# Three weight loads of the opening issued by ScalarE instead of the sync engine, in a graph-network kernel

## The chip, the cores and the metric

The program runs on one core of a Trainium2 chip. The metric is the device time of one execution in microseconds (us). Below, PE is TensorE's matmul side and PEld its weight load, DVE is VectorE, ACT is ScalarE, POOL is GpSimd and SP is the sync engine. "SPq" and "ACTq" are the instruction streams of SP and ACT where they issue transfers.

## What is computed

Four layers, each followed by a residual sum and a layer norm, over 32 graphs of 256 nodes with 256 features and one 256 x 256 adjacency. The first is a gated recurrent graph layer of three steps. The opening, which this change is about, is its first step on the first two graphs:

```python
h = x
for _ in range(T):                       # T = 3
    a_in = jnp.einsum('nm,bmd->bnd', in_mat, h)      # in_mat = out_mat = adj
    a_out = jnp.einsum('nm,bmd->bnd', out_mat, h)
    av = jnp.concatenate([a_in, a_out], axis=-1)
    z = sigmoid(_lin(av, w3_w, w3_b) + _lin(h, u3_w, u3_b))
    r = sigmoid(_lin(av, w4_w, w4_b) + _lin(h, u3_w, u3_b))
    hv = tanh(_lin(av, w5_w, w5_b) + _lin(r * h, u5_w, u5_b))
    h = (1.0 - z) * h + z * hv
```

Then come a linear attention-like layer with Wq, Wk, Wv, and two graph convolutions (weights called w2 and w3s in the kernel, with biases).

## The kernel before

Each engine has an instruction list written out by hand; semaphores join them. The graphs go in 16 pairs. A pair's data is 128 partitions x 1024 floats (512 KB). Two pairs are in flight: one in the "front" lane (tiles `f_...`, state `hf_...`) and one in the "back" lane (`b_...`, `hb_...`). Each engine runs `start()`, a loop, and `finish()`. Every fp32 product is made of three products of a high and a low part: ACT copies the high part (`..._hi`), DVE subtracts it from the source (`..._lo`), PE multiplies.

The opening loads the adjacency, the first pair, all weights and the bias rows. Their landing places are tiles that are free at that time, and the trace calls them by those names:

| transfer | tile in the trace | KB |
|---|---|---|
| adj | adj_nat | 256 |
| first pair | x_front | 512 |
| u3 | b_cand (first half) | 256 |
| w4 | b_z | 512 |
| w3 | b_gate | 512 |
| w5 | b_kept | 512 |
| u5 | b_cand (second half) | 256 |
| wv, w2 | normed | 256 each |
| wq, wk | hb_feat | 256 each |
| five bias vectors | bias_rows | 1 each |

In time, PE does this at the start: 13 transposes of the identity (L953), which nothing reads; `prepare(0)`, which transposes adj (L519); `turn_first`, which transposes the pair (L544); `prepare(1)`, which transposes u3 (L519); `mix(front, 0, k)`, 24 matmuls of adj with the pair (L489); `base`, the products with u3; the bias rows' transpose (L526); `prepare(2)` to `prepare(5)` for w4, w3, w5, u5, between products. `mix` needs `hf_node_lo`, which DVE makes (L1515) from `hf_node_hi`, which ACT makes from x_front. ACT's list opens with the bias transfers (L967), a table load, `prep_hi(0)` (adjT_hi), then two copies of x_front to `hf_node_hi`. DVE halves w4, w3 and w5 in place first (`sum_halves`, L1408).

POOL waits for w5's load before it issues `bias_out`:

```python
pool.wait_ge(s_load["w5"], 16)
```

SP's list is, after the loads, the second pair's load, its 32 x 32 blocks (`x_blocks`), and a copy of the state (`input_t`).

Of the kernel before, what the change touches and what calls it, by code (L numbers as in the profile page):

```python
# [21 lines left out]
P = 128  # L22
# [133 lines left out]
def build(nc, x, adj, w3_w, w3_b, u3_w, u3_b, w4_w, w4_b, w5_w, w5_b, u5_w, u5_b, wq, wk, wv,  # L156
# [14 lines left out]
    with ExitStack() as ctx:  # L171
# [3 lines left out]
        def sem(name):  # L175
            return ctx.enter_context(nc.semaphore(name))
# [83 lines left out]
        w3_nat, w4_nat, w5_nat = back.gate[:], back.z[:], back.kept[:]  # L260
        flat = lambda t: t[:].rearrange("p g c d -> p (g c) d")
        halves = lambda t: (t[:, 0].rearrange("p (c d) -> p c d", c=C), t[:, 1].rearrange("p (c d) -> p c d", c=C))
        u3_nat, u5_nat = halves(back.cand)
# [6 lines left out]
        s_load = {n: sem("s_load_" + n) for n in ("adj", "u3", "w4", "w3", "w5", "u5", "qk", "v", "l23", "bias", "bias_out")}  # L270
# [10 lines left out]
        def upto(n, k=1):  # L281
            return 2 * n + k + 1


        def ln(q, j, g):
            return 8 * q + 2 * j + g + 1
# [14 lines left out]
        def later(n):  # L301

            return not (isinstance(n, int) and n == 0)
# [4 lines left out]
        @block.sync  # L308
        def _(sp):
            def rows(w):  # L310
                return w.rearrange("(c p) d -> p c d", p=P)

            sp.dma_start(adj_nat[:], rows(adj)).then_inc(s_load["adj"], 16)
            sp.dma_start(x_front[:], x_pairs[0]).then_inc(s_x_front, 16)
            sp.dma_start(u3_nat, rows(u3_w)).then_inc(s_load["u3"], 16)
            sp.dma_start(w4_nat, rows(w4_w)).then_inc(s_load["w4"], 16)
            sp.dma_start(w3_nat, rows(w3_w)).then_inc(s_load["w3"], 16)
            sp.dma_start(w5_nat, rows(w5_w)).then_inc(s_load["w5"], 16)
            sp.dma_start(u5_nat, rows(u5_w)).then_inc(s_load["u5"], 16)
            sp.dma_start(wv_nat, rows(wv)).then_inc(s_load["v"], 16)  # L320
            sp.dma_start(wq_nat, rows(wq)).then_inc(s_load["qk"], 16)
            sp.dma_start(wk_nat, rows(wk)).then_inc(s_load["qk"], 16)
            sp.dma_start(w2_nat, rows(l2_w)).then_inc(s_load["l23"], 16)
            sp.dma_start(w3s_nat, rows(l3_w)).then_inc(s_load["l23"], 16)

            def load_front(p):

                if not later(p - 1):
                    sp.wait_ge(s_in_turned, upto(0))
                sp.wait_ge(state_f.s_node_lo, upto(2 * p - 2))  # L330
                sp.dma_start(x_front[:], x_pairs[p]).then_inc(s_x_front, 16)

            def load_blocks(p):

                if later(p - 1):
                    sp.wait_ge(state_f.s_feat, upto(2 * p - 2))
                for b in range(4):
                    sp.dma_start(x_blocks[32 * b:32 * b + 32].rearrange("k c (r i) -> k c r i", i=32),
                                 x_turnable[p, b]).then_inc(s_x_blocks, 16)

            def keep_input(p):

                sp.wait_ge(state_f.s_feat, upto(2 * p))
                if later(p):
                    sp.wait_ge(main.s_residual, upto(p - 1))
                sp.dma_start(input_t[:], state_f.feat[:]).then_inc(s_input_t, 16)

            def keep_last_input():

                sp.wait_ge(state_f.s_feat, upto(2 * LAST))  # L350
                sp.wait_ge(state_f.s_node_lo, upto(2 * LAST))
                sp.dma_start(last_pair.input_t, state_f.feat[:]).then_inc(s_input_t, 16)

            def move_blocks(S, turn):

                sp.wait_ge(S.s_blocks, 2 * turn)
                sp.dma_start(S.scratch.rearrange("b i a n -> (b i) a n"), S.blocks).then_inc(S.s_written, 16)
                sp.wait_ge(S.s_written, 16 * turn)
                for a in range(4):
                    sp.dma_start(S.moved[32 * a:32 * a + 32],  # L360
                                 S.scratch[:, :, a].rearrange("b i n -> i b n")).then_inc(S.s_moved, 16)

            def move_sum(Y, q):

                sp.wait_ge(Y.s_sum_blocks, upto(q))
                sp.dma_start(Y.scratch.rearrange("b i a n -> (b i) a n"), Y.sum_blocks).then_inc(Y.s_sum_written, 16)
                sp.wait_ge(Y.s_sum_written, 16 * q + 16)
                for a in range(4):
                    sp.dma_start(Y.sum_moved[32 * a:32 * a + 32],
                                 Y.scratch[:, :, a].rearrange("b i n -> i b n")).then_inc(Y.s_sum_moved, 16)  # L370

            def store(Y, q):
                sp.wait_ge(Y.s_normed, ln(q, 3, 1))
                sp.dma_start(out_pairs[q + Y.pair_before], Y.result[:]).then_inc(s_stored, 16)

            def store_graph(Y, q, g):
                sp.wait_ge(Y.s_normed, ln(q, 3, g))
                sp.dma_start(out_pairs[q + Y.pair_before][:, g], Y.result[:, g]).then_inc(s_stored, 16)

            load_front(1)  # L380
            load_blocks(1)
            keep_input(0)
            with sp.Fori(1, LAST) as p:
                load_front(p + 1)
                load_blocks(p + 1)
                keep_input(p)
                move_sum(main, p - 1)
                move_blocks(state_f, p)
                store(main, p - 1)
            keep_last_input()  # L390
            for Y, q, g in ((main, LAST - 1, 0), (last_pair, 0, 0), (main, LAST - 1, 1), (last_pair, 0, 1)):
                store_graph(Y, q, g)
            sp.wait_ge(s_stored, 16 * (PAIRS + 2))
# [568 lines left out]
        def _(act):  # L962
            def copy(dst, src):
                return act.activation(dst, src, ACT.Copy)  # L964

            for i, b in enumerate((w3_b, u3_b, w4_b, w5_b, u5_b)):
                act.dma_start(bias_rows[C * i:C * i + C], b.rearrange("(c p) -> c p", p=P)).then_inc(s_load["bias"], 16)  # L967

# [1162 lines left out]
```

## Time and profile before

| | us |
|---|---|
| median of 3 runs (1244.99 to 1246.29) | 1244.99 |
| profiled execution, its own time | 1243.87 |
| span of the profiled execution | 1242.1 |
| PE busy | 1221.6 (98%) |
| DVE busy | 1047.6 (84%) |
| ACT busy | 607.4 (49%) |
| POOL busy | 193.0 (16%) |

The span runs from the first to the last instruction; the time of an execution is a little more. A busy share is an average over the whole span. Times in the rows below count from the start of the span.

### The profile page before, as it was taken

Reading aid. Unit: us, or ns where it says so; the run is one execution under the profiler, and the core shown is the slowest. Engines: PE = TensorE matmul, PEld = TensorE weight load, DVE = VectorE, ACT = ScalarE, POOL = GpSimd, SP = SyncE. Lnnn points to the kernel's source line nnn. Section 1 sums busy time; section 2 is a strip of 40 time slices with the busy share of each in tenths; the row PEclk is TensorE's granted clock in tenths of the full one; section 3 lists DMA queues with packets and bytes.
Section 4 is the critical chain, followed back from the end, with each engine's and each line's share of the span. In section 5 each row is a group of like instructions: output and inputs, shape, how many; then the busy total and the mean of one; then the engine's idle time right before and its main releaser. Section 6 shows DMA issues by size and latency. Waiting matters only on the chain.

```text
span 1242.1 us, 21043 instructions
## 1 busy us (share of the span) xinstructions
PE 1221.6 (98%) x7454; PEld 1080.8 (87%) x7454; DVE 1047.6 (84%) x2332; ACT 607.4 (49%) x1067; POOL 193.0 (16%) x334
## 2 busy tenths in 40 slices
PE   8899999999999999999999999999999999999997
PEld 7788888888988989888888888989889898898896
DVE  6679888897988979888898888979889798894899
ACT  5445545545545444544555455455454445454542
POOL 1001021020211202112020210202112020110022
PEclk9999999999999999999999999999999999999999
DMA  6021210303103031220302104031030302200001
GB/s 203 18 69 35 76 61 18 116 3 99 36 34 101 0 101 34 51 84 17 90 28 78 57 17 117 1 101 34 34 101 0 101 34 51 84 17 17 1 2 35
DMA packets 105021, 66.93 MB, mean 54 GB/s; under 512 B 65690, under 2 KB 98468, under 8 KB 104996
## 3 DMA queue, kind: packets, MB, share of 16 engines
q1 hardware_dynamic: 104784, 66.08, 17.9%
q0 software_dynamic: 192, 0.52, 0.2%
q8 instruction: 15, 0.25, 0.1%
q14 instruction: 10, 0.08, 0.0%
q10 hardware_dynamic: 20, 0.01, 0.0%
HBM read 35.13 MB, written 23.07 MB: 47 GB/s over the span
## 4 chain that ended last, share of the span: by engine, by line
PE 95%; DVE 3%; POOL 1%; DMA 1%; ACT 0%; issue 0%; SPq 0%; DVEq 0%; ACTq 0%
PE b_ps L489 47%; PE f_ps L489 45%; PE f_ps L615 1%; PE b_ps L662 1%; DMA b_cand<-in_L_gnn_u_w 1%; DVE f_stats L1559 0%; DVE b_stats L1559 0%; DVE b_a_lo L1605 0%; PE b_ps L519 0%; DVE normed L1579 0%; DVE f_ps L1600 0%; DVE f_rh_lo L1605 0%; POOL b_rstd L410 0%; DVE hf_feat L1579 0%; DVE result L1579 0%
## 5 line engine op out<-in xcount | busy, mean ns | idle before, releaser
L408 POOL TENSOR_TENSOR b_var_eps<-b_moments,eps 128x2 f32<-128x2 f32 x120 | 44.3, 369 | 916.5 <-DVE b_moments L1566 916.5
L1016 ACT ACTIVATE f_cand<-f_ps,bias_c 128x512 f32<-128x512 f32 x66 | 45.5, 690 | 91.2 <-PE f_ps L489 91.2
L410 POOL TENSOR_TENSOR b_rstd<-b_var_eps,neg_half 128x2 f32<-128x2 f32 x120 | 88.1, 734 | 9.4
L964 ACT ACTIVATE f_a_hi<-f_ps 128x512 fp32r<-128x512 f32 x66 | 39.5, 598 | 94.3 <-PE f_ps L489 94.2
L964 ACT ACTIVATE b_rh_hi<-b_ps 128x512 fp32r<-128x512 f32 x90 | 53.8, 598 | 64.8 <-PE b_ps L489 64.8
L1442 DVE TENSOR_TENSOR f_gate<-f_gate,hf_feat 128x512 f32<-128x512 f32 x66 | 45.5, 689 | 46.7 <-ACT f_gate L1004 46.5
L964 ACT ACTIVATE b_a_hi<-normed 128x512 fp32r<-128x512 f32 x60 | 38.0, 633 | 94.5 <-DVE normed L1579 93.1
L489 PE MATMUL f_ps<-adjT_hi,hf_node_hi 128*128 128x256 f32 x264 | 75.1, 284 | 1.1 <-DVE hb_node_lo L1495 1.1
L489 PE MATMUL f_ps<-adjT_lo,hf_node_hi 128*128 128x256 f32 x264 | 73.7, 279 | 0.0
L489 PE MATMUL f_ps<-adjT_hi,hf_node_lo 128*128 128x256 f32 x264 | 73.6, 279 | 0.0
L1004 ACT ACTIVATE f_gate<-f_ps,bias_r 128x512 f32<-128x512 f32 x66 | 45.2, 686 | 51.3 <-PE f_ps L489 51.3
L1605 DVE TENSOR_TENSOR b_rh_lo<-b_ps,b_rh_hi 128x512 fp32r<-128x512 f32 x90 | 61.1, 679 | 2.7 <-ACT b_rh_hi L964 2.7
L1458 DVE TENSOR_TENSOR f_cand<-f_z,f_cand 128x512 f32<-128x512 f32 x66 | 45.6, 691 | 16.9 <-ACT f_cand L1016 15.8
L1436 DVE TENSOR_TENSOR f_a_lo<-f_ps,f_a_hi 128x512 fp32r<-128x512 f32 x66 | 44.8, 682 | 16.0 <-ACT f_a_hi L964 14.1
L964 ACT ACTIVATE f_rh_hi<-f_gate 128x512 fp32r<-128x512 f32 x66 | 41.4, 627 | 30.0 <-DVE f_gate L1442 30.0
L1012 ACT ACTIVATE f_z<-f_ps,bias_z 128x512 f32<-128x512 f32 x66 | 45.0, 683 | 20.2 <-PE f_ps L489 20.0
L489 PE MATMUL f_ps<-hf_feat_hi,u3T_hi 128*128 128x512 f32 x132 | 53.6, 406 | 0.7 <-DVE hf_feat_lo L1490 0.7
L489 PE MATMUL f_ps<-f_a_hi,w4T_hi 128*128 128x512 f32 x132 | 53.9, 408 | 0.0
L1442 DVE TENSOR_TENSOR b_gate<-b_gate,hb_feat 128x512 f32<-128x512 f32 x30 | 20.7, 688 | 38.6 <-ACT b_gate L1004 38.6
L489 PE MATMUL f_ps<-f_a_hi,w34T_hi 128*128 128x512 f32 x132 | 52.3, 396 | 0.9 <-ACT f_gate L1004 0.9
L489 PE MATMUL f_ps<-f_a_hi,w5T_hi 128*128 128x512 f32 x132 | 52.2, 396 | 0.0
L489 PE MATMUL f_ps<-f_a_hi,w34T_lo 128*128 128x512 f32 x132 | 52.2, 396 | 0.0
(337 smaller groups left out, 4608.1 us busy)
## 6 DMA issues: line engine op xcount, KB each, us to landing
x_front<-in_x SPq DMA_DIRECT2D x16, 512.0 KB, 3.5
x_blocks<-in_x SPq DMA_DIRECT2D x60, 128.0 KB, 3.5
input_t<-hf_feat SPq DMA_DIRECT2D x15, 512.0 KB, 2.9
turn_sum<-normed SPq DMA_DIRECT2D x14, 512.0 KB, 2.6
result<-turn_sum SPq DMA_DIRECT2D x56, 128.0 KB, 3.0
turn_f<-f_gate SPq DMA_DIRECT2D x14, 512.0 KB, 2.7
f_z<-turn_f SPq DMA_DIRECT2D x56, 128.0 KB, 2.9
out<-result SPq DMA_DIRECT2D x14, 512.0 KB, 3.0
```

The lines of the kernel that those rows point to most:

```text
L408: pool.tensor_tensor(Y.var_eps[:, g], Y.moments[:, g, :, 1], eps[:], ALU.add).then_inc(Y.s_var, 1)
L410: pool.tensor_tensor(Y.rstd[:, g], Y.var_eps[:, g], neg_half[:], ALU.pow).then_inc(Y.s_rstd, 1)
L489: last = pe.matmul(bank, s, m, start=start and i == 0, stop=stop and i == len(terms) - 1, skip_group_check=True)
L615: last = pe.transpose(ps1[:, g, c * D + k * P:c * D + (k + 1) * P], feat[:, k, g * N + c * P:g * N + (c + 1) * P], ident[:])
L964: return act.activation(dst, src, ACT.Copy)
L1004: act.activation(L.gate[:, k], L.ps0[:, k], ACT.Sigmoid, bias=bias_r[:, k:k + 1]).then_inc(L.s_r, 1)
L1012: act.activation(L.z[:, k], L.ps0[:, k], ACT.Sigmoid, bias=bias_z[:, k:k + 1]).then_inc(L.s_z, 1)
L1016: act.activation(L.cand[:, k], L.ps1[:, k], ACT.Tanh, bias=bias_c[:, k:k + 1]).then_inc(L.s_tanh, 1)
L1436: dve.tensor_tensor(L.a_lo[:, k], L.ps1[:, k], full(L.a_hi[:, k]), ALU.subtract).then_inc(L.s_a_lo, 1)
L1442: dve.tensor_tensor(L.gate[:, k], L.gate[:, k], L.state.feat[:, k], ALU.mult).then_inc(L.s_rh, 1)
L1458: dve.tensor_tensor(L.cand[:, k], L.z[:, k], L.cand[:, k], ALU.mult).then_inc(L.s_zc, 1)
L1605: dve.tensor_tensor(lo[:, g], src, full(hi[:, g]), ALU.subtract).then_inc(done, 1)
```

## The change

ACT issues the loads of w3, w5 and u5, as the first instructions of its list. SP no longer issues them. Destination, source, semaphores and everything that waits for them stay.

```diff
@@ sync engine
             sp.dma_start(x_front[:], x_pairs[0]).then_inc(s_x_front, 16)
             sp.dma_start(u3_nat, rows(u3_w)).then_inc(s_load["u3"], 16)
             sp.dma_start(w4_nat, rows(w4_w)).then_inc(s_load["w4"], 16)
-            sp.dma_start(w3_nat, rows(w3_w)).then_inc(s_load["w3"], 16)
-            sp.dma_start(w5_nat, rows(w5_w)).then_inc(s_load["w5"], 16)
-            sp.dma_start(u5_nat, rows(u5_w)).then_inc(s_load["u5"], 16)
             sp.dma_start(wv_nat, rows(wv)).then_inc(s_load["v"], 16)
@@ scalar engine
+            def rows(w):
+                return w.rearrange("(c p) d -> p c d", p=P)
+
+            act.dma_start(w3_nat, rows(w3_w)).then_inc(s_load["w3"], 16)
+            act.dma_start(w5_nat, rows(w5_w)).then_inc(s_load["w5"], 16)
+            act.dma_start(u5_nat, rows(u5_w)).then_inc(s_load["u5"], 16)
             for i, b in enumerate((w3_b, u3_b, w4_b, w5_b, u5_b)):
                 act.dma_start(bias_rows[C * i:C * i + C], b.rearrange("(c p) -> c p", p=P)).then_inc(s_load["bias"], 16)
```

The head of ACT's list in the kernel before, up to the copies of the first pair:

```order
1 L967 DMA bias_rows<-in_L_gnn_w_b 2x128
2 L967 DMA bias_rows<-in_L_gnn_u_b 2x128
3 L967 DMA bias_rows<-in_L_gnn_w_b 2x128 x2
4 L967 DMA bias_rows<-in_L_gnn_u_b 2x128
5 L964 ACT_TABLE_LOAD
6 L964 ACTIVATE adjT_hi<-b_ps 128x512
7 L964 ACTIVATE hf_node_hi<-x_front 128x512 x2
```

The same place in the changed kernel (b_gate is w3, b_kept is w5, b_cand is u5):

```order
1 L966 DMA b_gate<-in_L_gnn_w_w 128x2x512
2 L967 DMA b_kept<-in_L_gnn_w_w 128x2x512
3 L968 DMA b_cand<-in_L_gnn_u_w 128x2x256
4 L970 DMA bias_rows<-in_L_gnn_w_b 2x128
5 L970 DMA bias_rows<-in_L_gnn_u_b 2x128
6 L970 DMA bias_rows<-in_L_gnn_w_b 2x128 x2
7 L970 DMA bias_rows<-in_L_gnn_u_b 2x128
8 L961 ACT_TABLE_LOAD
9 L961 ACTIVATE adjT_hi<-b_ps 128x512
10 L961 ACTIVATE hf_node_hi<-x_front 128x512 x2
```

Three transfers of 1280 KB now stand ahead of the five bias transfers and of the table load. The head of SP's list in the changed kernel (b_cand is u3, b_z is w4):

```order
1 L313 DMA adj_nat<-in_adj 128x2x256
2 L314 DMA x_front<-in_x 128x4x256
3 L315 DMA b_cand<-in_L_gnn_u_w 128x2x256
4 L316 DMA b_z<-in_L_gnn_w_w 128x2x512
5 L317 DMA normed<-in_L_gnn_Wv 128x2x256
6 L318 DMA hb_feat<-in_L_gnn_Wq 128x2x256
7 L319 DMA hb_feat<-in_L_gnn_Wk 128x2x256
```

Its first four transfers are those of before; wv follows w4 directly, where w3, w5 and u5 stood between them. The lists of PE, DVE and POOL are unchanged.

## Rows read from the trace of the kernel before

**Rows 1.** The page: span, and busy time, share and instructions by engine.

```profile
span 1242.1 us, 21043 instructions
PE 1221.6 (98%) x7454; PEld 1080.8 (87%) x7454; DVE 1047.6 (84%) x2332; ACT 607.4 (49%) x1067; POOL 193.0 (16%) x334
```

**Rows 2.** Chain that ended last, opening: start, duration, what.

```profile
1.75 6.41 DMA b_cand<-in_L_gnn_u_w
8.20 0.66 PE b_ps L519 x4
```

**Rows 3.** Timeline, SP's issues: start, duration, instruction.

```profile
0.75 0.44 SPq L313 DMA_DIRECT2D adj_nat<-in_adj  x1
1.25 0.45 SPq L314 DMA_DIRECT2D x_front<-in_x  x1
...
2.83 0.47 SPq L317 DMA_DIRECT2D b_gate<-in_L_gnn_w_w  x1
...
4.37 0.89 SPq L320 DMA_DIRECT2D normed<-in_L_gnn_Wv  x1
```

**Rows 4.** Issues by transfer: KB, and us from issue to landing.

```profile
adj_nat<-in_adj SPq DMA_DIRECT2D x1, 256.0 KB, 2.9
x_front<-in_x SPq DMA_DIRECT2D x1, 512.0 KB, 3.9
...
b_gate<-in_L_gnn_w_w SPq DMA_DIRECT2D x1, 512.0 KB, 8.0
```

**Rows 5.** Timeline of PE: start, duration, instructions [idle before, releaser].

```profile
4.48 1.06 PE L519 MATMUL b_ps<-ident,adj_nat 128*128 128x128 f32 x4
5.33 1.33 PE L544 MATMUL f_ps<-ident,x_front 128*128 128x128 f32 x8
...
8.61 0.36 PE L489 MATMUL f_ps<-adjT_hi,hf_node_hi 128*128 128x256 f32 x1
...
11.49 0.39 PE L489 MATMUL f_ps<-hf_feat_hi,u3T_hi 128*128 128x512 f32 x1
```

**Rows 6.** Timeline of ACT and DVE on the way to the first mix.

```profile
2.52 1.28 ACT L964 ACT_TABLE_LOAD   x1 [2.52 <-issue]
5.58 0.60 ACT L964 ACTIVATE adjT_hi<-b_ps 128x512 fp32r<-128x512 f32 x1 [1.77 <-PE b_ps L519]
6.07 1.14 ACT L964 ACTIVATE hf_node_hi<-x_front 128x512 fp32r<-128x512 f32 x2
6.82 1.28 DVE L1515 TENSOR_TENSOR hf_node_lo<-x_front,hf_node_hi 128x512 fp32r<-128x512 f32 x2
```

**Rows 7.** Windows: PE, PEld, DVE, ACT, POOL busy, granted clock, DMA share, GB/s.

```profile
3.00:4.00 1.00, 1.00 (x6) 1.00 (x6) 0.00 (x0) 0.81 (x1) 0.00 (x0) 1.00 1.09 378
5.00:6.00 1.00, 1.00 (x7) 0.98 (x6) 0.00 (x0) 0.42 (x1) 0.00 (x0) 1.00 0.94 205
...
1235.00:1238.00 3.00, 0.38 (x4) 0.17 (x2) 2.93 (x14) 0.00 (x0) 1.30 (x4) 1.00 0.24 87
1238.00:1242.00 4.00, 0.00 (x0) 0.00 (x0) 1.46 (x4) 0.00 (x0) 0.43 (x1) 0.52 0.58 197
```

**Rows 8.** ACT's DMA queue, whole span, 2.5 to 5, 5 to 7: packets, MB, share.

```profile
q10 hardware_dynamic: 20, 0.01, 0.0%
...
q10 hardware_dynamic: 12, 0.00, 0.5%
...
q10 hardware_dynamic: 4, 0.00, 0.7%
```

**Rows 9.** Timeline: ACT's last bias issue, DVE's first use of later loads.

```profile
2.22 0.28 ACTq L967 DMA_DIRECT2D bias_rows<-in_L_gnn_u_b  x1
11.11 0.68 DVE L1408 TENSOR_TENSOR b_z<-b_z 128x512 f32<-128x512 f32 x1
12.93 0.68 DVE L1408 TENSOR_TENSOR b_gate<-b_gate 128x512 f32<-128x512 f32 x1
...
17.05 1.27 DVE L1421 TENSOR_REDUCE row_sum<-hb_feat 128x2 f32<-128x512 f32 x2
```

## The prediction

> **What bounds the kernel now.** I read the page first. PE is busy for 98% of the span and nothing else is near it [rows 1], so the kernel is one long list of matmuls, and a change at its start counts only by how much later or earlier PE can begin its unbroken work. Everything behind is a chain on PE, so a shift of that point should come out at the end as it is; I take no discount for it.
>
> The chain of waits says what sets that point. From 1.75 us the chain is the transfer of u3, 6.41 us long, to 8.16; four transposes of u3 follow, and then the first matmuls [rows 2]. PE's timeline shows the same: it transposes adj and the pair up to 6.66, is idle, and starts the first mix at 8.61; its 24 matmuls last until the base product at 11.49 [rows 5]. But u3 is not the only thing that PE waits for there. The mix reads hf_node_lo, which DVE makes from 6.82 to 8.10 behind ACT's copies, and these began at 6.07, when ACT had done adjT_hi [rows 6]. So two inputs come at almost the same time: the node parts at 8.10 and u3 at 8.16. Whichever becomes later moves the mix.
>
> Then the transfers. SP issues one every 0.51 us from 0.75 to 4.37, w3 at 2.83 [rows 3]. With the times to landing [rows 4]: adj lands at 0.75 + 2.9 = 3.65, the first pair at 1.25 + 3.9 = 5.15, w3 at 2.83 + 8.0 = 10.83. The DMA engines are full while this goes on (share 1.09 at 3 to 4 us, 378 GB/s), with a dip to 205 GB/s at 5 to 6 us though still 0.94 busy [rows 7]. So transfers are served in the order of the queue, at full bandwidth, and w3, w5 and u5 stand behind everything that the first mix needs.
>
> **The change, part by part.** *Removed from SP:* three issues at about 0.51 us, so wv and all behind it are issued 1.5 us earlier. The earliest reader of them is DVE at 17.05, without a wait [rows 9]. Worth nothing.
>
> *Added to ACT ahead of its own work:* three issues, 1.5 us at SP's pace. The table load goes from 2.52 to about 4.0 and ends at about 5.3; ACT's first work starts at 5.58, and it waited 1.77 us for it [rows 6]. Hidden, with 0.3 us to spare, and more when the pair lands later (below). If an issue cost twice as much on ACT, adjT_hi would be 1.2 us late, still ahead of the copies by then.
>
> *The bias rows* stand behind 1280 KB in ACT's queue. Even at the end of all that, some 9 us, they are ahead of their use behind the base product, which starts at 11.49 [rows 5]. Nothing.
>
> *The order at the DMA engines:* this is what the change does. w3 (512 KB) is now handed over at 0.75, together with adj, then w5 at about 1.25 and u5 at 1.75, in a queue of their own. If the two queues take turns, they take bandwidth from adj, the pair and u3, when there is none left over. What the turns look like: ACT's last bias transfer is issued at 2.22 [rows 9], yet of its 20 packets 12 move from 2.5 to 5 and the last 4 after 5 [rows 8]. So small packets of ACT's queue wait for their turn behind many of SP's, but get it: the engine takes neither all of SP's first nor one packet each. I take turns of about one transfer's share.
>
> The Trainium skill, page "DMA: Bandwidth & Descriptors", section "Queues, rings and completion order", says that each engine goes round between its queues and drains some 9 to 17 descriptors from one before it switches. The rows agree as far as they go. By that rule the pair would land behind 1792 to 2048 KB, by turns of equal bytes behind 1536 KB.
>
> With turns of one share each, the pair needs two turns of SP (it has twice adj's rows) after adj's one. If SP's queue begins, w3 and w5 come in between: 256 + 512 + 512 + 512 = 1792 KB until the pair is in. If ACT's begins, u5 too: 2048 KB. Before, it was 768 KB at 5.15.
>
> When does that land? Lower bound: adj to pair was 512 KB in 1.50 us, 341 KB/us. From 5.15, 1024 KB more gives 8.15 and 1280 KB more 8.9. Upper bound: before, w3's landing closed the same 2048 KB, and came at 10.83. The difference of 2 us is the dip at 5 to 6 us, with some engines late behind it; u3, only 256 KB behind the pair, landed 3.0 after it where 0.75 would do.
>
> From the pair's landing L the rest is in rows: ACT's copies began at 6.07 and hf_node_lo was done at 8.10, 2.03 later; a mix needs 0.05 more. Before, the mix's start was 8.61, less the 0.03 for its weight load. So the delay is L + 2.08 - 8.58 = L - 6.5. No dip: 8.15 to 8.9 gives 1.65 to 2.4. Dip ahead of the pair: 10.83 gives 4.3. Dip between the pair and u3: u3 lands at L + 3.0, its transposes take 0.43 of PE's time (8.20 to 8.61, [rows 2, 5]), the mix starts at L + 3.43, and the delay is 3.0 to 3.75. I take L = 9.5, halfway between 8.15 and 10.83: **3.0 us** later.
>
> *Later loads.* w4 now has 2816 KB ahead of it and itself, where before it was 1536. At 341 KB/us from 5.15 that is 11.2, with the 2 us of the dip 13.2; DVE used it at 11.11 [rows 9] and will come to it 3 us later, at 14.1. Hidden by 0.9 to 2.9. If that cover were gone, w4's preparation would be late one for one. w3, used at 12.93 [rows 9], and w5 behind it come earlier. POOL's wait for w5 ends earlier, and its bias_out joins the queues; nothing reads it soon.
>
> **Sum.** Profiled execution: span 1242.1 + 3.0 = 1245.1, own time 1243.87 + 3.0 = 1246.9. The median of the runs, 1244.99, is 1.1 above that execution, so I forecast 1244.99 + 3.0 = 1248.0, bounds 1.65 and 4.3: 1246.6 to 1249.3.
>
> **Rivals.** *TensorE's clock falls in the longer idle stretch (0.22).* The four transposes of adj at 4.48 took 1.06 us, those of u3 at 8.20 only 0.66; the granted clock reads 1.00 over the opening, yet the early ones ran at half the pace (0.85 us to the next group against 0.41) [rows 2, 5]. At the end of the kernel the granted clock is 1.00 until 1238 and 0.52 after, some 3 us behind the last matmul [rows 7]; that is the 1.2 GHz level. Before, PE's idle stretch was 1.5 us and the clock survived. Now it is from about 6, when adj's transposes end, to 9.5: 3.5 us. From its first work at 1.65 PE was slow until between 5.33 and 6.66, about 4.3 us. If it starts slow at L, it is slow until L + 4.3, of which the last 2.2 us lie in the mix at half pace: 1.1 us more; if only the mix's start counts, 2.1. Delay 4.1 to 5.1, to 1249.1 to 1250.1; with the upper L, 6.
>
> *Turns of equal bytes (0.13).* The pair would then land behind 1536 KB: 7.4 at 341 KB/us, delay 0.9, up to 1.6 with a little of the dip: 1245.9 to 1246.6, within 0.2%. For it: nothing; the packets of [rows 8] are too small to tell.
>
> *Not slower (0.13).* SP's queue stays in front, since ACT's transfer of 128 partitions needs longer to get going, or turns favour SP. Then the pair lands at 5.15 as before. u3 without w3 behind it could come earlier, but the node parts hold the mix at 8.15, against 8.58: 0.43 us is all that can be won, 1244.6. It decides if the pair lands before 6.07, where ACT is free for it. Against it: ACT's first packets were served as early as SP's, 4 of 20 having moved by 2.5 us [rows 8]. The Trainium skill, same page, section "Issuing engines are not separate DMA queues", holds that issuing from several engines saves sequencer time alone. By that the time is 1244.6 to 1245.5; the trace shows that sequencer time is not short here.
>
> **How the numbers follow.** My forecast has 0.52. A measurement of this kernel can tell about 0.2%, 2.5 us. Of the forecast's delays 1.65 to 4.3, two thirds are above that: 0.35; the clock adds 0.22. Slower 0.57, faster 0.03 (more than the 0.43 that I can find), same 0.40. The range leaves out a delay under 0.4 (0.1) and over 5.6 (0.06): 1245.4 to 1250.6.
>
> **What would show it.** x_front's landing grows from 3.9 to 7 to 9.5 us, adj's from 2.9 to 4 or so, w3's falls from 8.0 below 5.5; hf_node_hi starts at the pair's landing; the first mix starts at 10.3 to 13; PE's idle stretch before u3's transposes splits into one ahead of the pair's transposes and one ahead of the mix. Behind the mix every interval is as before. Wrong if x_front lands by 6, if the mix starts late but PE makes it up behind, or if w4 or the bias rows become a wait of their own.

## The result, and the profile after

| | before | changed |
|---|---|---|
| median of 9 runs, us | 1244.99 (1243.43 to 1246.29) | 1248.82 (1246.85 to 1249.48) |
| span of the profiled execution, us | 1242.1 | 1245.0 |
| own time of the profiled execution, us | 1243.87 | 1246.86 |

The change makes the kernel slower: the ratio is 1.0028, with a 95% interval of 1.0019 to 1.0036. That is 3.5 us. (The two medians differ by 3.8 and the lowest times by 3.4; the runs of both kernels lie in groups, see e9 to e12.)

The chain of waits of the changed kernel (start, duration, what) has another transfer in its first place than [rows 2]:

```profile
0.75 0.43 SPq L313
1.19 0.06 issue
1.25 7.49 DMA x_front<-in_x
8.73 0.04 issue
8.78 1.97 PE f_ps L541 x8
10.75 0.85 PE b_ps L516 x4
11.60 4.36 PE f_ps L486 x30
```

The first pair, x_front, now lands at 8.74 instead of 5.15, and PE waits for it. The issues with their times to landing, changed kernel:

```profile
adj_nat<-in_adj SPq DMA_DIRECT2D x1, 256.0 KB, 3.7
b_gate<-in_L_gnn_w_w ACTq DMA_DIRECT2D x1, 512.0 KB, 4.4
b_kept<-in_L_gnn_w_w ACTq DMA_DIRECT2D x1, 512.0 KB, 7.2
x_front<-in_x SPq DMA_DIRECT2D x1, 512.0 KB, 7.5
b_cand<-in_L_gnn_u_w SPq DMA_DIRECT2D x1, 256.0 KB, 8.4
b_cand<-in_L_gnn_u_w ACTq DMA_DIRECT2D x1, 256.0 KB, 8.1
```

With the issue times (0.75 for adj and w3, 1.25 and 1.29 for the pair and w5, 1.74 and 1.80 for u3 and u5), adj lands at 4.45, w3 at 5.15, w5 at 8.5, the pair at 8.74, u5 at 9.9 and u3 at 10.1. Set beside [rows 4]: w3, which nobody needs before DVE reads it at 15.84, gained 5.7 us, and the pair lost 3.6. The two queues of the changed kernel from 5 to 7 us (packets, MB, share of 16 engines) show how they share:

```profile
q10 hardware_dynamic: 221, 0.45, 58.2%
q1 hardware_dynamic: 303, 0.31, 45.2%
```

ACT's queue (q10) carries w5 in rows of 2 KB, SP's (q1) the pair in rows of 1 KB. Both move at the same time. From 4 to 5, 6 to 7 and 7 to 8 us they move nearly the same number of packets (127 and 121, 129 and 127, 180 and 182), from 5 to 6 us not (92 and 176). So ACT's larger packets take more than half of the bytes. Up to 8.74 us, when the pair lands, ACT's queue has moved 1.30 MB, nearly all of its 1280 KB, and SP's 1.02 MB; up to the pair's landing before, at 5.15, it was 0.96 MB in all. PE's timeline of the changed kernel, against [rows 5]:

```profile
4.62 0.81 PE L516 MATMUL b_ps<-ident,adj_nat 128*128 128x128 f32 x4
8.78 1.97 PE L541 MATMUL f_ps<-ident,x_front 128*128 128x128 f32 x8 [3.35 <-DMA x_front<-in_x]
10.54 1.06 PE L516 MATMUL b_ps<-ident,b_cand 128*128 128x128 f32 x4
11.25 0.56 PE L486 MATMUL f_ps<-adjT_hi,hf_node_hi 128*128 128x256 f32 x1
```

The first mix starts at 11.25 where it was 8.61. The idle stretch ahead of the pair's transposes is 3.35 us, and in it TensorE's clock fell. Windows of the changed kernel, columns as in [rows 7]:

```profile
8.00:9.00 1.00, 0.22 (x1) 0.22 (x2) 0.00 (x0) 0.24 (x1) 0.25 (x1) 0.71 1.12 365
9.00:10.00 1.00, 1.00 (x6) 1.00 (x6) 0.58 (x1) 0.98 (x3) 1.00 (x2) 0.50 1.04 373
...
11.00:12.00 1.00, 1.00 (x7) 1.00 (x6) 0.91 (x2) 0.38 (x2) 0.07 (x1) 0.58 1.10 348
```

The granted clock (the third number from the end) is 0.50, the 1.2 GHz level, from 8.4 to 11.8. The pair's 8 transposes took 1.97 us where a full clock gives 1.09 (below), and u3's 1.06 instead of 0.66. ACT's timeline, against [rows 6]:

```profile
4.31 1.28 ACT L961 ACT_TABLE_LOAD   x1 [4.31 <-issue]
5.60 0.60 ACT L961 ACTIVATE adjT_hi<-b_ps 128x512 fp32r<-128x512 f32 x1
8.76 1.15 ACT L961 ACTIVATE hf_node_hi<-x_front 128x512 fp32r<-128x512 f32 x2 [2.56 <-DMA x_front<-in_x]
```

adjT_hi starts at 5.60 as before (5.58): ACT's longer list of issues cost nothing, though the table load ends just as adjT_hi can begin. A point further on, the eight matmuls of L531 (L534 before), begins at 32.31 instead of 29.40, 2.91 later, and the span is 2.9 longer. Nothing is made up behind the opening.

### The profile page after: what moved, and what is told of

It is laid out like the page before. It is cut to its first block, busy times and chain, and to the rows that moved or that the text cites. A ratio compares the mean times of both kernels' runs of the same rounds, so it can differ in the third digit from the quotient of the medians.

```text
span 1245.0 us, 21043 instructions
## 1 busy us (share of the span) xinstructions
PE 1222.7 (98%) x7454; PEld 1081.7 (87%) x7454; DVE 1047.6 (84%) x2332; ACT 607.7 (49%) x1067; POOL 193.3 (16%) x334
## 4 chain that ended last, share of the span: by engine, by line
PE 95%; DVE 3%; DMA 1%; POOL 1%; ACT 0%; issue 0%; DVEq 0%; SPq 0%; ACTq 0%
PE b_ps L486 47%; PE f_ps L486 45%; PE f_ps L612 1%; PE b_ps L659 1%; DMA x_front<-in_x 1%; DVE f_stats L1562 0%; DVE b_stats L1562 0%; DVE b_a_lo L1608 0%; PE b_ps L516 0%; DVE normed L1582 0%; DVE f_ps L1603 0%; DVE f_rh_lo L1608 0%; POOL b_rstd L407 0%; DVE hf_feat L1582 0%; DVE result L1582 0%
## 5 line engine op out<-in xcount | busy, mean ns | idle before, releaser
L961 ACT ACTIVATE b_rh_hi<-b_ps 128x512 fp32r<-128x512 f32 x90 | 53.8, 598 | 64.8 <-PE b_ps L486 64.8
```

## The experiments

Each row's first mix and landing are from its own profile. Times are medians of 11 runs (e7: one) and ratios are to runs of the kernel before taken beside them, whose medians were 1244.80 (e1 to e4), 1245.32 (e5 to e8) and 1244.81 (e9 to e12). In e9 to e12, "16 transposes" stand near 52 us and "24 transposes" in the opening.

| kernel | pair lands | first mix | time | ratio to before, 95% |
|---|---|---|---|---|
| e1, only ACT's issues | 5.4 | 8.15 | 1243.49 | 0.9996 (0.9987 to 1.0005) |
| e2, GpSimd, behind the pair | 5.0 | 8.14 | 1244.89 | 1.0005 (0.9996 to 1.0014) |
| e3, change + 24 transposes | 8.65 | 10.65 | 1246.89 | 1.0019 (1.0010 to 1.0028) |
| e4, only w3 on ACT | 6.8 | 8.83 | 1245.24 | 1.0007 (0.9998 to 1.0016) |
| e5, only u5 on ACT | 5.8 | 8.14 | 1244.91 | 0.9993 (0.9984 to 1.0002) |
| e6, the pair on ACT | 5.45 | 8.15 | 1243.55 | 0.9991 (0.9982 to 1.0001) |
| e7, before again | 5.2 | 8.15 | 1243.37 | one run |
| e8, ACT, behind its copies | 5.75 | 8.12 | 1245.13 | 0.9996 (0.9987 to 1.0005) |
| e9, before + 16 transposes | 5.4 | 8.51 | 1243.87 | 0.9992 (0.9983 to 1.0001) |
| e10, e6 + 16 transposes | 5.35 | 8.16 | 1243.44 | 0.9986 (0.9977 to 0.9996) |
| e11, change + 16 transposes | 8.55 | 11.10 | 1246.94 | 1.0022 (1.0013 to 1.0031) |
| e12, change + 16 and 24 | 8.65 | 10.86 | 1247.00 | 1.0017 (1.0008 to 1.0026) |

The theory: the two queues share the full DMA engines, so the pair lands late, and the idle stretch that this makes lowers TensorE's clock. Rivals: ACT's later start; a cost of the second queue wherever it comes in time; a clock that costs nothing.

**e1: ACT's issue time alone.**

```diff
+            for i in range(3):
+                act.dma_start(spare[:, :, 4 * i:4 * i + 4], rows(adj)[:, :, 4 * i:4 * i + 4]).then_inc(s_spare, 16)
             for i, b in enumerate((w3_b, u3_b, w4_b, w5_b, u5_b)):
```

(The spare tile, its semaphore and SP's wait for it at the end of the program are left out here.)

> All loads stay with SP; ACT issues three transfers of 128 partitions and 4 KB each ahead of its bias rows, so it spends the issue time of the change and moves no bytes to speak of. Theory (the pair lands late because the queues share bandwidth): the pair lands near 5.2 us, the first mix starts near 8.6, time within 0.1% of before. Rival (ACT's later start is the cause): the first mix starts over 1 us later, most of the 2.9 us is here.

ACT's table load started at 4.22, about where the change has it, and the mix at 8.15. The delay isn't in ACT's list. This rival falls. The run shows one thing more: up to 5.35 us, when the pair landed, ACT's queue had moved 672 packets, but only 0.01 MB in them. In the changed kernel it was 800 packets and 1.30 MB by the pair's landing. With so many packets in the second queue the pair landed 0.2 us later than in the profile before, within the spread of such landings (e2 to e8, below); with their bytes it landed 3.6 us later. So it is the bytes, and not the number of packets.

**e2: the same three loads, out of SP's list, but behind the pair.**

```diff
-            sp.dma_start(w3_nat, rows(w3_w)).then_inc(s_load["w3"], 16)
...
+            pool.wait_ge(s_x_front, 16)
+            pool.dma_start(w3_nat, rows(w3_w)).then_inc(s_load["w3"], 16)
```

(w5 and u5 likewise.)

> w3, w5 and u5 leave SP's list as in the change, but GpSimd issues them, and only once the pair has landed. Theory: the pair lands by 5.2 us, PE's clock stays up, the first mix starts at 8.2 to 8.7, time within 0.1% of before. Rival (taking the loads out of SP's list costs by itself, or a second queue slows everything): 2 us or more slower.

The pair landed 3.8 us after its issue and the mix started at 8.14. Taking the loads from SP costs nothing that the times resolve, and neither does another queue that starts late.

**e8: the loads in ACT's queue, but behind its copies of the pair.**

```diff
                 for k in range(2):
                     input_nodes_hi(0, k)
+                act.dma_start(w3_nat, rows(w3_w)).then_inc(s_load["w3"], 16)
```

(w5 and u5 likewise; none of them at the head of the list.)

> The three loads are issued by ACT, but behind its copies of the pair to hf_node_hi instead of first. Theory: the pair lands by 5.2 us and the first mix starts as before or 0.4 us sooner (8.2 to 8.6); ACT's next copies come 1.5 us later, which may hold the base product by up to 1.2 us; time +0 to +1.2 us, clock stays up. Rival (loads on ACT's queue cost wherever they stand): +2.5 us or more.

The mix started at 8.12, time as before. The same loads in the same queue, 5 us later, don't delay the first mix. The pair was expected by 5.2 and landed at 5.75, though none of the three loads was issued before 5.80. The three issues stand in ACT's way, as expected: its next copy began at 7.65 instead of 7.11, and L531 begins at 29.52 where e7 has 28.95. These 0.6 us, within the expected 1.2, are in the trace; the times don't resolve them.

**e4 and e5: a part of the bytes.** e4 has only w3 at the head of ACT's list, e5 only u5; the rest stays with SP.

> Only w3 (512 KB) is issued by ACT, first. Theory: the pair lands behind 256 + 512 + 512 = 1280 KB, 5.15 + 512/341 = 6.65 us, 0.6 us after ACT is free for it; the first mix starts at 9.2 at most, +0.1 to +0.6 us in all, clock stays up. Rival (any big load in ACT's queue costs the full amount): pair at 8 us or more, +2.5 us.

> Only u5 (256 KB) is issued by ACT, first. Theory: the pair lands behind 1024 KB, at 5.9 us, still ahead of 6.07, where ACT is free for it; first mix at 8.6 at most, time within 0.1% of before. Rival (any big load in ACT's queue costs): pair over 7 us, +1 us or more.

The issue rows of the pair in e4:

```profile
x_front<-in_x SPq DMA_DIRECT2D x1, 512.0 KB, 5.5
```

and in e5:

```profile
x_front<-in_x SPq DMA_DIRECT2D x1, 512.0 KB, 4.5
```

So the pair landed at 5.75 with 256 KB beside it, 6.75 with 512 KB and 8.55 to 8.74 with 1280 KB; expected were 5.9 for 256 and 6.65 for 512. With no bytes to speak of beside it, it landed at 5.0 to 5.75 (e2 and e8), so e5's 5.75 doesn't show a price by itself; e4's and the changed kernel's landings are clear of that spread. A late landing counts only from 6.07 on, where ACT is free for the pair: e5's mix was not late, e4's was by 0.68 us, and its clock stayed up (granted clock 1.00, the pair's transposes 1.09 us). e4's ratio is +0.9 us, above the forecast of at most +0.6, but its interval holds no change at all as well.

**e6: the pair's load on ACT, all else with SP.**

> The kernel before, but ACT issues the pair's load, first, and SP all else. Theory (one packet each in turn): the pair's 32 packets per engine share with adj's 16 and u3's 16, so adj lands near 4.0, pair and u3 both near 6; PE is no longer held by u3 (8.16 before), but by the node parts, first mix at 8.1 to 8.3, 0.3 to 0.5 us less than before, too little for the timing. Rival (turns are by whole transfers, SP's first): w4 gets between and the pair lands at 7 or later, first mix at 9.5 or later, +1 us.

The pair landed at 5.45 and u3 at 6.1, so u3 no longer held the mix, which started at 8.15, with DVE's node parts as its last wait. The theory's order was right; the pair landed earlier than I expected, u3 as expected.

**e7: the kernel before, once more.** It asks whether the late u3 of [rows 2] is chance.

> The kernel before, profiled once more. If the dip to 205 GB/s at 5 to 6 us and the late landings behind it belong to the order of the loads, u3 lands near 8.2 again; if they are chance, u3 lands near 6 and the first mix starts at 8.2.

Its dip is there again, in a window of this kernel:

```profile
5.00:6.00 1.00, 1.00 (x9) 0.94 (x8) 0.00 (x0) 0.43 (x1) 0.00 (x0) 1.00 0.89 206
```

and u3's transposes started at 7.63, not 8.20. The dip stays, how late it makes u3 varies: neither of the two expectations fits whole. In this execution u3 hid behind the node parts, and the mix was at 8.15. The 8.61 of the profile before thus has 0.46 us in it that not every execution has.

**e3: the clock's share.** The changed kernel, with PE kept at work.

```diff
                 prepare(0)
+                for _ in range(24):
+                    pe.transpose(front.ps1[:, 1, 0:P], ident[:], ident[:])
                 turn_first(0)
```

> The changed kernel, with 24 more transposes of the identity on PE ahead of the pair's transposes, which nothing reads. Theory of two parts (the pair's landing is 2.1 us of the delay, the fallen clock the other 0.8): granted clock 1.00 through the opening, pair still at about 8.7 us, first mix at 10.8, 0.8 us faster than the change (1.0022 of before against 1.0028). Rival (the clock costs nothing, the pair alone is the delay): same time as the change, 1.0028 of before.

PE's timeline of e3:

```profile
4.98 2.78 PE L853 MATMUL f_ps<-ident 128*128 128x128 f32 x24
8.66 1.09 PE L541 MATMUL f_ps<-ident,x_front 128*128 128x128 f32 x8 [0.89 <-DMA x_front<-in_x]
10.07 0.65 PE L516 MATMUL b_ps<-ident,b_cand 128*128 128x128 f32 x4 [0.32 <-DMA b_cand<-in_L_gnn_u_w]
10.65 0.39 PE L486 MATMUL f_ps<-adjT_hi,hf_node_hi 128*128 128x256 f32 x1
```

At the full clock the pair's transposes take 1.09 us, the mix starts 0.60 earlier than in the changed kernel, and L531 begins at 31.48 instead of 32.31: 0.83 us less. PE now waits for u3 itself. In this trace the clock was worth 0.8 us, as expected. By the medians of the timed runs, 1.0019 against 1.0028, it is not resolved: the intervals overlap, and e3's runs lie in groups too.

**e9 to e12: the second place where the clock falls.** The runs of before lie in groups: of its first 9, three are at 1243.4 to 1243.5 and six from 1244.8 to 1246.3. The profiled executions of e5 and e6 (own times 1244.91 and 1244.94) and of e8 (1246.31) had a fall of the clock near 54 us that those of before, e1, e2 and e7 (1243.87 the first, 1243.4 the others) have not. The mean granted clock of single runs says the same: of the 33 runs of before beside e9 to e12, the 16 up to 1244.15 have 0.998 or 0.999, the 17 from 1244.81 on 0.995 to 0.997. Windows of e6 (the kernel before is idle there from 51.5 to 52.7 and from 53.8 to 54.9):

```profile
52.00:54.00 2.00, 1.09 (x8) 0.86 (x8) 1.41 (x4) 1.63 (x3) 0.00 (x0) 1.00 0.16 54
54.00:56.00 2.00, 1.54 (x8) 1.57 (x9) 2.00 (x4) 0.60 (x2) 0.00 (x0) 0.66 0.00 0
56.00:58.00 2.00, 2.00 (x11) 2.00 (x11) 0.71 (x2) 0.00 (x0) 0.00 (x0) 0.50 0.00 0
```

So I filled these two stretches in the kernel before (e9), in e6 (e10), in the changed kernel (e11) and in e3 (e12). The cut shows e9; in e12 the 24 transposes of e3 stand in the opening besides.

```diff
                 prepare(8)
+                pe.wait_ge(s_prep_lo, 8)
+                for _ in range(8):
+                    pe.transpose(back.ps1[:, 1, 0:P], ident[:], ident[:])
                 for k in range(2):
                     turn_h(state_b, 0, k)
+                for _ in range(8):
+                    pe.transpose(back.ps1[:, 1, 0:P], ident[:], ident[:])
```

> The kernel before, with 16 transposes of the identity on PE in its two idle stretches at 51.5 and 53.8 us, which nothing reads. Theory (the groups of times at 1243.4 and at 1244.8 and over are runs without and with a fall of PE's clock near 54 us): all runs at 1243.3 to 1243.9, none over 1244.5. Rival (the groups have another cause): runs spread to 1246 as for the kernel before.

> The pair's load first in ACT's list, all else with SP, and the 16 filling transposes at 51.5 and 53.8 us. Theory: first mix at 8.15, all runs at 1243.3 to 1243.5, median 1.5 us under that of before (0.9988 of it). Rival: as the pair's load on ACT without the transposes, spread to 1245.5.

All 11 runs of e9 lie from 1243.45 to 1244.08, a little above the expected 1243.9 at the upper end, and all of e10 from 1243.00 to 1243.51, where the same chip's runs of the kernel before reached from 1243.34 to 1247.12. A window of e10 at the place of e6's fall:

```profile
54.00:56.00 2.00, 1.80 (x16) 1.60 (x14) 2.00 (x5) 0.56 (x2) 0.00 (x0) 1.00 0.00 0
```

The clock stays at 1.00 and the groups are gone. e10 is the one version here that is faster than the kernel before beyond its interval, by 0.14% (0.04 to 0.23%). Its median is 0.43 us under e9's, with the mix at 8.16 against 8.51 in the profiles: that is what the pair's load on ACT is worth, because u3 no longer comes last. The other 0.9 us between the medians goes with the clock near 54 us.

> The changed kernel with the 16 filling transposes. Theory: all runs near 1246.9, which is 3.4 over the filled kernel before (3.1 us by the first mix, 11.25 against 8.15, and 0.3 for its first matmuls at the slow clock). Rival (the change's cost is also in the later fall): 1246 or less, or spread to 1249.

> The changed kernel with the 16 filling transposes and with the 24 ahead of the pair's. Theory: granted clock 1.00 through the opening, first mix at 10.65, all runs near 1245.9, 1.0 less than with the 16 alone; the rest, 2.5 us over the filled kernel before, is the landing of the pair and of u3 alone. Rival (the clock of the opening costs nothing): the same time as with the 16 alone.

e11's median is 3.07 us over e9's, the cleanest measure of the change that I have. It was expected at 3.4, with the mix at 8.15 before; e9's profile has it at 8.51, near the profile before (8.61), and 3.07 + 0.36 is 3.4. e11's runs still spread, 1246.54 to 1248.04, for its opening is still open to the clock. PE's timeline of e11:

```profile
8.63 1.97 PE L541 MATMUL f_ps<-ident,x_front 128*128 128x128 f32 x8 [2.99 <-DMA x_front<-in_x]
11.10 0.56 PE L486 MATMUL f_ps<-adjT_hi,hf_node_hi 128*128 128x256 f32 x1
```

The transposes take 1.97 us again, and the matmuls of the mix stay slow until 13.6 (0.41 us each, 0.28 afterwards), where the changed kernel's were fast from 11.8. L531 is at 33.09, 0.8 later than in the changed kernel, though the mix is earlier. The granted clock reads 1.00 in this profile all the while, so here only the durations show the slow stretch.

e12 missed in time and not in span. By its trace it is faster than e11 (mix at 10.86, L531 at 31.66), and so are the spans of all its runs: 1243.9 to 1244.3, median 1244.1, against 1244.7 to 1246.2, median 1245.1, in e11. That is the 1.0 us that was expected. By its times it is not faster: 1247.00 against 1246.94. What lies outside the span is 2.4 to 3.1 us in e12's 11 runs, where it is 1.8 to 1.9 in e9, e10, e11, the changed kernel and the kernel before. The trace has a lead: one packet of the instruction queue (q8, 0.02 MB) moves at 1246.2, after the last instruction of the span at 1244.3, and no other trace here has one there. Whether this transfer is what the time outside the span grew by, no run isolates.

So the clock's share in the opening is shown, 1.0 us in the spans of 11 runs each (e12 against e11) and 0.8 us in e3's trace. e3's five lowest runs agree, with spans of 1243.9 to 1244.1, where the changed kernel has none under 1245.0. The rest of the change, from e9's median span of 1242.1 to e12's 1244.1, is 2.0 us and is left for the landings of the pair and of u3. In e12 the gain of the clock does not reach the measured time.

## Why the prediction was right, and where not

**Direction and size.** Forecast +3.0 us, 1248.0, range 1245.4 to 1250.6; measured 1248.82, +3.5 by the ratio, +3.07 from e9 to e11. The step that carries it is shown by e1, e2, e4 and e8: it is the bytes in a second queue, issued while the first is full, that make the pair late.

**The landing of the pair.** I took L = 9.5, halfway between a landing without and with the dip. It was 8.74, within the bound without a dip (8.15 for 1792 KB, 8.9 for 2048 KB). By then 1.36 MB more had moved than at the pair's landing before, all but a little of ACT's 1280 KB among it, so the case is that of 2048 KB. The error is in the choice of L: the dip to 205 GB/s did not come. The changed kernel moves 369 GB/s from 5 to 6 us, and so do its kin, from 357 (e12) to 383 (e3), e4 with 377, and the two with the pair in ACT's queue (e6 356, e10 382). The kernel before and e1, e2, e5, e7, e8 and e9 have the dip, from 130 (e9) to 272 GB/s (e1). In these 14 profiles it goes with the order of the loads: it is absent in the seven in which ACT's queue carries 512 KB or more from the start. What in the order causes it no run settles.

**The turns.** I assumed equal turns, a transfer's share each. The order of landing (adj, w3, w5, pair, u5, u3) fits ACT's three shares against SP's, a share being 16 rows for each DMA engine. The bytes from 5 to 7 us, 0.45 against 0.31 MB, show that the turns are not by equal bytes. That they are by equal numbers of packets fits three of the four microseconds from 4 to 8, and how long one turn is no run here shows.

**The delay from the landing.** L - 6.5 gives 2.24 for 8.74. The node parts were done at 9.42 + 1.29 = 10.71, so the mix could have started at 10.76; it started at 11.25. The rest, 0.5 us, is the rival that I gave 0.22: the clock fell, and the transposes ran late. Some 0.3 more went in the first matmuls (mix to L531: 21.06 us, against 20.79 before). I had priced it at 1.1 to 2.1; it was 0.8 in this profile, since the clock was back at 11.8, before 8.74 + 4.3. It varies: between the profiles of e11 and e12 L531 differs by 1.4. So an overestimate of the landing (0.8) and a rival that I left out of the sum (0.8) cancelled. That the sum came out within half a microsecond is luck in this respect; the direction and the mechanism are not.

**The baseline.** The profile's own 8.61 holds 0.46 us for u3 that e7, e1 and e2 don't have. Against them the mix is 3.1 later, and that with 0.3 for its slow start is the distance between the lowest times of both kernels, 1246.85 and 1243.43. I had found those 0.43 us, as the most that could be won, but not that the kernel before often has them already.

**What was costed at nothing** held: ACT's issues (e1; adjT_hi at 5.60 against 5.58, though the table load ended at 5.59 and not at 5.3, so nothing of the 0.3 us to spare was left), the bias rows, SP's earlier issues, w4 (landed at 11.5, within my 11.2 to 13.2; DVE takes it at 13.86 without a wait). *Not slower* (0.13) fell with the landing rows, and *turns of equal bytes* (0.13), which had the pair at 7.4, with the 8.74. The Trainium skill's section "Issuing engines are not separate DMA queues" (page "DMA: Bandwidth & Descriptors") says that transfers issued by several engines run on the same 16 DMA engines and interleave, and that only sequencer time is saved. The traces agree: 358 GB/s at 3 to 4 us with two queues, 378 with one. That the second queue does no harm either would be the wrong reading, and there *not slower* went wrong: the interleaving changes whose bytes come first.

## What to carry to other kernels

In this kernel the DMA engines are full while the opening loads. Then the order of a single queue works as a priority list, and moving later loads to a second queue gives them a share of the bandwidth ahead of what is needed first. So price such a move by the bytes that newly come ahead of the most urgent transfer, and count only what exceeds the time at which its reader is free; to use the second queue safely, put the urgent transfer in it (e6, e10: the pair itself came no earlier, at 5.35 to 5.45, but u3 did, and e10 has 0.43 us less than e9), or start it when the urgent one has landed (e2), or about then (e8). And look what the longer idle stretch does to TensorE's clock.

## What I had not expected of the hardware

Two idle stretches of little over 1 us each, 51.5 to 52.7 and 53.8 to 54.9 us in the profile before, are enough in some executions to bring TensorE down to the 1.2 GHz level (granted clock 0.50 from 56 to 58 us in e6) and not in others (1.00 in e7). The lowest times of before and the group 1.5 us above differ by that: the mean granted clock of a run tells the two groups apart, and with 16 transposes that nothing reads no run of e9 and e10, 22 in all, was in the upper group. A kernel of 1245 us that seems noisy by 0.2% may have such a place.
